# Second layer of a two-layer attention kernel: ScalarE copies a finished unit's sums ahead of the step's first exponential

## The reference, cut to what matters

```python
    x = _L0_conv_ref(x, ...)                       # pooled keys, mixture of two softmaxes, + residual
    # second layer, for each image and head:
    xn = (x - mean) / jnp.sqrt(var + EPS) * gamma
    q, k, v = jnp.split(jnp.einsum('oc,bcn->bon', w_qkv, xn), 3, axis=1)
    sim = jnp.einsum('bhdi,bhdj->bhij', q, k) * scale + bias[None]
    attn = softmax(sim)                            # over the 3136 keys j
    out = jnp.einsum('bhij,bhdj->bhdi', attn, v)
    return jnp.einsum('oc,bcn->bon', w_out, out) + residual
```

## Time and profile before

| | |
|---|---|
| three runs | 3760.82, 3760.3, 3749.16 us, median 3760.3 us |
| profiled execution | 3773.08 us, its span 3771.3 us |
| PE busy | 3555.4 us, 94% |
| DVE busy | 2797.6 us, 74% |
| ACT busy | 2315.8 us, 61% |
| POOL busy | 849.0 us, 23% |
| mean granted clock of TensorE | 0.938 of full speed |
| second layer's steps | about 1387 to 3752 us of the span |

### The profile page before, as it was taken

How to read it: one execution, slowest core, us unless ns; L and a number is a source line. 1 busy time by engine, 2 the same in 40 slices (tenths; PEclk the granted TensorE clock), 3 DMA queues, 4 the chain that set the end, 5 groups by cost and what they waited for, 6 DMA issues and landing times.

```text
span 3771.3 us, 70851 instructions
## 1 busy us (share of the span) xinstructions
PE 3555.4 (94%) x27690; PEld 1087.8 (29%) x27690; DVE 2797.6 (74%) x8284; ACT 2315.8 (61%) x2830; POOL 849.0 (23%) x935
## 2 busy tenths in 40 slices
PE   6998998999998899999999999999999999999997
PEld 2222222222222223333333223333333333333332
DVE  5567767777776678877887777788887788888870
ACT  2566657666668436666666666656666656666665
POOL 2144334333432512022111012210102211100000
PEclk6789889988889869999999999999999999999999
DMA  1188887600000312332233222223322233233221
GB/s 54 15 54 55 57 53 57 48 16 17 21 12 13 78 39 78 84 88 70 71 83 96 73 73 73 74 74 92 89 74 70 76 89 79 73 89 87 77 59 28
DMA packets 268053, 236.35 MB, mean 63 GB/s; under 512 B 222184, under 2 KB 225112, under 8 KB 267464
## 3 DMA queue, kind: packets, MB, share of 16 engines
q1 hardware_dynamic: 241544, 205.85, 29.0%
q0 software_dynamic: 26176, 25.98, 3.3%
HBM read 226.65 MB, written 27.19 MB: 67 GB/s over the span
## 4 chain that ended last, share of the span: by engine, by line
PE 80%; DVE 9%; issue 7%; ACT 2%; POOL 1%; DMA 1%; POOLq 0%; SPq 0%; ACTq 0%; DVEq 0%
PE P L731 26%; PE P L716 16%; PE P L684 11%; PE P L697 9%; DVE maxes L1051 7%; PE P L673 5%; PE P L757 5%; PE P L807 2%; PE P L701 2%; PE P L784 1%; ACT probs L940 1%; PE P L773 1%; PE P L819 1%; ACT L989 0%; POOL high L539 0%
## 5 line engine op out<-in xcount | busy, mean ns | idle before, releaser
L940 ACT ACTIVATE probs<-P 128x896 f32<-128x896 f32 (+1 forms) x2352 | 2044.3, 915 | 1265.2 <-PE P L716 872.7
L1070 DVE CUSTOM_DVE_ANT_0 junk<-P,mstage 112x448 bf16<-112x448 f32 x3136 | 1830.0, 622 | 460.0 <-PE P L684 455.3
L731 PE MATMUL P<-probs,vals 128*17 128x448 f32 (+1 forms) x9408 | 1181.8, 576 | 23.4 <-ACT sums L1016 22.8
L1051 DVE TENSOR_REDUCE maxes<-P 128x1 f32<-128x392 f32 (+1 forms) x1600 | 796.4, 558 | 336.8 <-PE P L673 336.0
L716 PE MATMUL P<-bstage,flip 112*56 112x448 f16 x6272 | 740.6, 358 | 0.0
L684 PE MATMUL P<-keys,q_stack 48*112 48x448 f16 x3136 | 622.9, 380 | 4.1 <-DVE maxes L1070 3.9
L697 PE MATMUL P<-q_two,keys 49*128 49x448 f16 x3136 | 560.9, 355 | 15.3 <-ACT probs L940 15.3
L673 PE MATMUL P<-keys,q_stack 24*128 24x392 f16 (+1 forms) x1600 | 415.2, 367 | 84.7 <-DVE maxes L1051 52.3
L539 POOL TENSOR_SCALAR high<-projected,cst 128x448 f16<-128x448 f32 x112 | 157.0, 1402 | 1247.4 <-ACT projected L949 1203.0
L716 PEld LDWEIGHTS P<-bstage,flip 112*56 112x56 f16 x6272 | 277.4, 106 | 351.2 <-issue 226.8
L697 PEld LDWEIGHTS P<-q_two,keys 49*128 49x128 f16 x3136 | 150.8, 93 | 716.3 <-ACT probs L940 645.1
(11 more groups left out here) (129 smaller groups left out, 1440.3 us busy)
## 6 DMA issues: line engine op xcount, KB each, us to landing
mstage<-g_max SPq DMA_DIRECT2D x56, 1519.0 KB, 8.0
bstage<-g_bias SPq DMA_DIRECT2D x28, 1568.0 KB, 8.1
bstage<-g_bias SPq DMA_DIRECT2D x28, 1519.0 KB, 8.6
g_max<-t_bf SPq DMA_DIRECT2D x16, 673.8 KB
keys<-d_rden POOLq DMA_DIRECT2D x42, 224.0 KB, 6.1
rwide<-d_rden POOLq DMA_DIRECT2D x42, 224.0 KB, 4.7
g_bias<-t_hi SPq DMA_DIRECT2D x8, 679.9 KB
g_bias<-t_lo SPq DMA_DIRECT2D x8, 679.9 KB
```

What stands on the lines that cost most here:

```text
L731: last = mm(P[32 * h:32 * h + HD + 1, PV, 0:QB], table[0:kr, kt, h, :], probs[0:kr, s % 3, h, :], start=kt == 0, stop=kt == unit.tiles - 1 ...
L940: A(probs[0:kr, s % 3, 2 * p:2 * p + 2, :], P[0:kr, 2 * p:2 * p + 2, 0:QB], ACT.Exp).then_inc(exp_done, 1)
L1051: V.tensor_reduce(out=maxes0[0:size, unit.i % 2, t, HALVES[r], c:c + 1], in_=P[0:size, bank_of(job), 0:HALF], op=ALU.max, axis=AX.X).then_ ...
L1070: V.tensor_tensor_reduce(out=junk[:, PLAN.nth[job] % 4, :], in0=P[0:QT, bank_of(job), 0:QB], in1=bias, scale=1.0, scalar=-3.0e38, op0=ALU. ...
```

## The change

In steps of the second layer the copy of the finished sums stands ahead of the step's first exponential instead of between its two exponentials. Steps of the first layer, and the copy after the last unit, stay as they were. No instruction is added or removed.

```diff
             for s in range(-PRE, LAST + POST):
                 for p, w in enumerate("ab"):
-                    if 0 <= s < LAST:
+
+                    sums_first = 0 <= s < LAST and STEPS[s][0].biased
+                    if 0 <= s < LAST and not sums_first:
                         exponentials(s, p)
                     for j in at_stage("copied", s) if p == 0 else []:
                         act.wait_ge(pv_done, s - 1)
...
                         elif j >= SLOW + 2:
                             act.wait_ge(scaled_made, j - 1)
                         A(sums_of(j), P[:, PV, 0:QB], ACT.Copy).then_inc(sums_made, 1)
+                    if sums_first:
+                        exponentials(s, p)
                     beside(s, w)
```

## The result

The changed kernel took 3721.3 us in the median of 20 runs (3700.0 to 3746.1); the kernel before, run beside it 20 times, 3749.4 us (3727.8 to 3769.5). The ratio is 0.9921, with an interval from 0.9900 to 0.9942: faster by 0.8%, 28.1 us between the medians. The prediction said 24.6 us less, which is 0.9934 and inside the interval, and 3735.7 us, which is 14.4 us too high; the median lies 0.7 us under the low end of the range.

What follows compares the result with a forecast made beforehand. It took TensorE to set the second layer's pace, pausing at unit boundaries for the copy of the sums. 26 x 0.90 + 0.79 + 0.42 = 24.6 us, so 3760.3 - 24.6 = 3735.7 us; range 3722 to 3750.

Steps and rivals of the forecast that it cites:

- The place and the price of the pause: Second-layer unit boundaries: TensorE's `values` waits for the copy of the sums; removing this gives 0.90 us at each of 26.
- The spare time: ScalarE ahead of the first exponential: the moved copy fits in 1.03 us of idle time with 0.70 us to spare.
- What is late next: Step behind a boundary: `scores(s+1, 1)` waits for the second exponential as in ordinary 2.76 us steps, so all 0.90 goes.
- The last boundary: Boundary without first-pass pairs, where ScalarE sets the pace: step falls from 3.47 to 2.68 us, a gain of 0.79.
- The boundary with the layer norm: ScalarE's chain there starts 0.42 us sooner, gaining 0.42 us; TensorE's wait of 1.42 us falls to 1.0.
- Half speed behind the pauses: Clock fall behind the layer norm's 1.42 us wait: might stay away, gaining 0 to 1.7 us; taken as 0.
- the list of what the profile would show: Expected profile signs: no copy wait above 1 us, 2.76 us boundary steps, 1.0 us layer-norm wait, second layer 24 to 26 shorter.
- the last of the sum: Whole kernel: the 24.6 us gain taken from the earlier runs' median of 3760.3 us gives 3735.7 us.
- The sentence ahead of it: Median 3760.3 us lies 12.8 below the profiled execution; the difference was put in the first layer, with clock down to 0.81.
- ScalarE takes the pause over: Boundaries: a copy over 0.70 us late delays both exponentials, so `scores` waits instead; 0.50 too late gives 3750 us; chance 0.09.
- the kernel gets slower: Boundaries: a copy delayed 1.5 us beyond its spare time delays `scores` and gives 3777 us; chance 0.05.
- the pause does not matter: Second layer: TensorE has room and another engine's chain sets the pace, so no change, 3760 us; chance 0.05.

Runs made afterwards that it cites:

- e3_half: Changed kernel with the copy moved only at boundaries whose new unit is even-numbered (14 of 28); second layer 2349.8 us, against 2361.6 before without half speed.
- e4_late: Kernel before with the copy put behind the step's second exponential; second layer 2407.2 us, 2381.7 without half speed.
- e6_two_more: Changed kernel with two extra ScalarE copies between the moved copy and the first exponential, at 28 boundaries; second layer 2345.8 us without half speed.
- e5_one_more: Changed kernel with one extra ScalarE copy between the moved copy and the first exponential, at 28 boundaries; second layer 2337.0 us without half speed.
- e2_after: Changed kernel run again unaltered; second layer 2336.7 us without half speed, timed ratio to the kernel before 0.9932.
- e1_before: Kernel before, run again unaltered for its profile; second layer 2361.6 us without half speed.
- e7_last_unit: Changed kernel with `biases(s, 0)` ahead of `scores(s, 1)` in the last unit only; second layer 2331.6 us.
- e8_all_units: Changed kernel with `biases(s, 0)` ahead of `scores(s, 1)` in every step of the second layer; second layer 2492.1 us.

## Why the prediction missed, point by point

**The place and the price of the pause** were right. 0.90 us at each of 26 boundaries, nothing handed on: the second layer lost 25.0 us without what half speed costs, for a sum of 24.6. (With it, the first two profiles differ by 21.7 us, less than the 24 to 26 that the prediction wanted to see there.) e3_half shows that it is additive, e4_late that it is the copy's place that sets it.

**The spare time** was right: 0.70 us worked out, 0.69 from e6_two_more, and nothing lost in e5_one_more. The copy starts 0.09 us behind `values`, as the earlier trace rows had it. At the boundary with the layer norm there was less, 0.27 us of idle time.

**What is late next** was right. The weight load of `scores(s+1, 1)` waits as in an ordinary step, and the total of the waits of L697 is 15.3 us before and after.

**The last boundary**: a step of 2.68 us (3612.19 to 3614.87) instead of 3.47, as worked out:

```profile
3612.19 1.73 ACT L940 ACTIVATE probs<-P 128x896 f32<-128x896 f32 x2 [0.95 <-PE P L716]
3613.80 0.55 ACT L1018 ACTIVATE sums<-P 128x448 f32<-128x448 f32 x1
3614.87 1.73 ACT L940 ACTIVATE probs<-P 128x896 f32<-128x896 f32 x2 [0.52 <-PE P L716]
```

**The boundary with the layer norm**, after the change (it answers to the earlier trace rows):

```profile
2014.31 1.73 ACT L940 ACTIVATE probs<-P 128x896 f32<-128x896 f32 x2 [0.27 <-PE P L716]
...
2016.06 1.28 ACT L989 ACT_TABLE_LOAD   x1
...
2020.73 0.36 PE L697 MATMUL P<-q_two,keys 49*128 49x448 f16 x2 [1.17 <-ACT probs L940]
```

The copy fitted ahead of the exponential, but the wait fell only to 1.17 us, not to 1.0. From the first exponential to the end of the wait it is 6.42 us, for 6.86 before, so the chain is the 0.44 shorter that was worked out; but 0.19 of that does not show in the pause, since another short delay there went too: the second first-pass pair started 1.06 us behind `biases` before and 0.88 behind it now. A slip in the list of what the profile would show, not in the sum.

**Half speed behind the pauses**: I set it at 0, between 0 and 1.7 us of gain. In the profile after, it was 3.4 us of loss (6.8 us for 3.4). But it varies from one execution to the next, whatever the kernel: e2_after and e1_before have 5.1 each, e3_half and e7_last_unit none. Of the 17 such stretches in the profiles without the copy's longer pauses, 16 stand behind a wait of 1.06 to 1.42 us at the layer norm's table loads, sometimes behind one and sometimes behind another, and one (in e5_one_more) behind two waits of 0.67 and 0.39 us close together at the same place. The pauses that were removed had no part in it.

**The step that failed** is the last of the sum: "So the forecast is 3760.3 - 24.6 = 3735.7 us". I took the median of three runs as the level to start from, and gave it the spread of those three. The level was 3749.4 us over 20 runs, 10.9 us lower, and 10.9 + 25.0 makes 35.9 of the 39.0 us between 3760.3 and 3721.3; the other 3 us are within what 20 runs leave uncertain (standard deviation of the changed kernel's runs 12.4 us, so 2.8 for their mean). The sentence ahead of it was right and should have been used for the range: the granted clock of the first layer differs between executions. The prediction even named as a sign of its being wrong that the first layer's clock moves the whole by more than the second layer gives. In the two profiles it did, 42.6 us against 21.7; the profiled execution took 3708.7 us, for 3748.5 worked out. Over the 20 runs of the changed kernel the clock of the whole execution goes from 0.938 (3746.1 us) to 0.956 (3700.0 us), and time and clock have a correlation of -0.99. Three runs of a program whose runs spread over 46 us fix its median to some 10 us at best, and a range of 28 us round a level known so badly was too narrow. Why the first layer is granted more of its clock in one execution than in another stays open; it was not tried.

**The rivals.** That ScalarE takes the pause over, and that the kernel gets slower, need a copy that is late by over 0.70 and 1.6 us; at its 0.09 us behind `values` it was not late at all. That the pause does not matter fell with e3_half and e4_late. The weight loads of the second layer are busy for 735 of 2343 us after the change, 31% as before, and yet each pause of TensorE went into the time in full. The Trainium skill, Perfetto Trace Analysis, section Identifying the Most-Contended Engine, names this share as one of two measures of TensorE's headroom. Here the share did not tell whether a pause counts; the intervals between the starts of TensorE's groups did.

## What to carry to other kernels

On an engine that works in order, look at each instruction that another engine waits for and ask how long its own inputs have been ready: here the sums were ready for two microseconds while the copy stood behind an exponential that had to wait for later work. Move such an instruction to where the engine idles anyway, and check the idle time against its length, since everything behind it shares the rest. Where only one part of a program was changed, compare that part in the profiles: it showed 25.0 us to 0.2 us, where the whole time scattered over 46 us; and take no level from three runs.

## What the hardware showed that I had not expected

- A pause of TensorE of 1.64 us can be followed by a stretch at half speed (granted clock 0.59 over 4 us). In e4_late this came behind 11 of 26 such pauses and behind the one of 1.97 us, and made each of these 12 boundaries some 1.6 us longer still (2.3 to 2.4 us over the kernel before, for 0.81 elsewhere). All 65 pauses of 0.83 us in three profiles left the clock at 1.00. Those of 1.06 to 1.42 us, behind the layer norm's table loads, did either: none to four falls in a profile, and not at the same places.
- Cutting TensorE's eight bias matmuls in two groups with another shape between them, and the first of them behind a first-pass pair, cost 0.21 us a step, 161 us in 27 units. The list of waits shows nothing of it: TensorE's waits in the layer fell, from 18.3 us in the changed kernel to 5.9 in e8_all_units.
